# A decoder layer's first stage: eight value blocks copied to places of their own, and five products on zeros ahead of the first data

## The chip, the cores and the metric

The kernel runs on one core of one Trainium2 chip. The metric is the device time of one execution in microseconds, taken as the median of several. A core has five engines that run their own instruction streams and wait for each other by semaphores: TensorE (PE, with its weight loads shown as PEld), VectorE (DVE), ScalarE (ACT), GpSimd (POOL) and SyncE (SP, which here only issues transfers). All arithmetic is float32 in and out.

## What is computed

The reference is one pre-norm decoder layer on 32 sequences of 64 tokens with 512 features: self-attention with 32 heads, cross-attention with 32 query heads and 8 key/value heads of 128 on the context `ctx_4096`, and a linear layer with low-rank additions, each added to `x`. The part that matters here is the beginning of the cross-attention, which does not need `x` and stands first in the program: keys and values of the context, and the keys' rotary embedding.

```python
k = (key @ Wk).reshape(nb, q_len, KVH, D).transpose(0, 2, 1, 3)      # key = value = ctx, Wk, Wv: 512 x 1024
v = (value @ Wv).reshape(nb, q_len, KVH, D).transpose(0, 2, 1, 3)
cos = cos_t[position_ids][:, None]
sin = sin_t[position_ids][:, None]
k = k * cos + _rotate_half(k) * sin
```

## The kernel before

A float32 product is made of three products of "fp32r" parts: each operand is split into a high part (ACT copies with rounding, `*_hi`) and a low part (DVE subtracts, `*_lo`), and PE sums hi*hi, hi*lo and lo*hi over the four chunks of 128 features (`product3`, lines 75 to 77, twelve instructions of 128x512 each). Where a product is made on plain float32 instead, PE runs every written product as two instructions in the trace: lines 1835 and 1836 write 4 x 4 products of 256 columns for `p_ps_qk` and `p_ps_s` (NCH = 4 terms, KC = 4 chunks).

The first stage is class `KeysAndValues`. The 2048 tokens stand in four blocks of 512 (`NB`), the keys in 8 heads of 128 (`KVH`), and the values of a block in eight value blocks: 4 tiles of 128 tokens by 2 halves of 512 features. Every engine has a `first()` for block 0 and a `body(b)` for blocks 1 to 3; the order of the work is written out by hand in them.

For block 0 PE runs, in this order:
- `first_values` (lines 444 to 446): value blocks 0 to 3, chunk by chunk as context and weights come in, 48 instructions into four PSUM banks;
- `values(0, i)` for i = 4 to 7. Blocks 4 and 5 wait for `v_copied` of 1 and 2, blocks 6 and 7 for 5 and 6, since they write banks that blocks 4 and 5 used;
- `keys(0, 0)` and `keys(0, 1)`;
- after `id_in` and `row_in` (line 460: all 16 gathers of rotary rows must have landed) 32 transposes (line 465), four for each of eight halves of a cosine or sine table, in two banks by turns, each after ACT has copied out the one two before;
- `keys(0, i)` for i = 2 to 7.

ACT in block 0 copies value block i out of PSUM (`copy_values`, line 330) and after each splits key weights i (line 320), then copies the eight table parts (line 345), then splits the context of block 1 (line 309). `v_out` has two buffers: copy i waits for `v_stored[i % 2]`, that is, until the store of copy i - 2 into `v_scratch` has landed. SP issues, in order: the first context and value weights, eight key-weight loads (line 239, after `c_ready` of 4), eight stores of values (line 256), the context load of block 1 (line 271, 1 MB), and then stores of keys (line 251) and loads of `x`. POOL gathers the 16 sets of rotary rows (line 298), one behind the other, after the last value weight has landed. DVE makes the low parts, then `rotate(b, i)` (lines 169 to 171), which needs both table parts of its block; between the first rotations stand the four `context_lo(1, c)`.

`cos_t` and `sin_t` are two tables of 128 x 2048 each in SBUF. They are written first by the ACT copies of line 345, and read from `rotate(0, 0)` on.

Of the kernel before, what the change touches and what calls it, by code (L numbers as in the profile page):

```python
# [26 lines left out]
P = 128  # L27
# [146 lines left out]
class KeysAndValues:  # L174

    def __init__(self, nc, m, base, banks, x, norm1, ident, drams, wv1_hi, wv1_lo):
        x_dram, ident_dram, pos_dram, table_dram, ctx_dram, wk_dram, wv_dram, wv1_dram, k_scr, v_scr, cos_scr, sin_scr = drams
        NKV = KVH * D2
        NH = NKV // BLOCK  # L180
        KB = 1024

        def sb(name, at, shape, dt=F32):
            return nc.alloc_sbuf_tensor_at("p1_" + name, shape, dt, offset=base + at)
# [17 lines left out]
        def rows(t):  # L202
            return rows_of[t // (3 * TPB)][:, t % (3 * TPB), :]

        def values_bank(b, i):

            return ps_k[i % 2] if b == 0 and 2 <= i < TPB else ps_v[i % 2]
# [9 lines left out]
        c_part, c_ready = m.sem("p1_c_part"), m.sem("p1_c_ready")  # L217
        k_done, v_done, k_terms, k_added, v_copied = (m.sem("p1_" + n) for n in ("k_done", "v_done", "k_terms", "k_added", "v_copied"))
        k_stored, v_stored = [m.sem(f"p1_k_stored{i}") for i in range(2)], [m.sem(f"p1_v_stored{i}") for i in range(2)]
        wv1_in, wv1_part, wv1_ready = (m.sem("p1_" + n) for n in ("wv1_in", "wv1_part", "wv1_ready"))  # L220
        self.k_stored, self.tables_out, self.v_done, self.c_ready = k_stored, tables_out, v_done, c_ready
        self.row_copied, self.wv1_ready = row_copied, wv1_ready
# [7 lines left out]
        def sync(sp):  # L230
# [22 lines left out]
            def store_values(b, i):  # L253
                need(sp, v_copied, b * KVH + i + 1)
                t, g0 = i % TPB, (i // TPB) * (KVH // NH)
                sp.dma_start(v_scr[g0:g0 + KVH // NH, ds(b, 1), :, t, :].rearrange("g b p d -> p (g b) d"),
                             v_out[i % 2][:, :].rearrange("p (g d) -> p g d", d=D2)).then_inc(v_stored[i % 2], 16)

            def first():
                for i in range(KVH):  # L260
# [46 lines left out]
        def scalar(act, extra):  # L307
            def context_hi(b, c):
                nc.scalar.activation(c_hi[b % 2][:, c, :], c_raw[b][:, c, :], ACT.Copy).then_inc(c_part, 1)

            def value_weights_hi(n):
                h, c = n // KC, n % KC
                act.wait_ge(v_raw_in[n], 16)
                cols = slice(h * BLOCK, (h + 1) * BLOCK)
                nc.scalar.activation(w_hi["v"][:, c, cols], raw["v"][:, c, cols], ACT.Copy).then_inc(part_hi["v"], 1)

            def key_weights_hi(i):
                act.wait_ge(k_raw_in[i // 2], 32)
                cols = slice(i * D2, (i + 1) * D2)
                nc.scalar.activation(w_hi["k"][:, :, cols], raw["k"][:, :, cols], ACT.Copy).then_inc(part_hi["k"], 1)  # L320

            def own_value_weights_hi(c):
                need(act, wv1_in, 16)
                need(act, v_done, (NB - 1) * KVH)
                nc.scalar.activation(wv1_hi[:, c, :], wv1_raw[:, c, :], ACT.Copy).then_inc(wv1_part, 1)

            def copy_values(b, i):
                need(act, v_done, b * KVH + i + 1)
                need(act, v_stored[i % 2], (b * (KVH // 2) + i // 2) * 16)
                nc.scalar.activation(v_out[i % 2][:, :], values_bank(b, i)[:, :], ACT.Copy).then_inc(v_copied, 1)  # L330

            def first():
                for c in range(KC):
                    act.wait_ge(c_in0[c], 16)
                    context_hi(0, c)
                    value_weights_hi(c)
                for c in range(KC):
                    value_weights_hi(KC + c)
                for i in range(KVH):
                    copy_values(0, i)  # L340
                    key_weights_hi(i)
                for n in range(2 * NB):
                    act.wait_ge(row_turned, n + 1)
                    dst = (cos_t, sin_t)[n % 2]
                    nc.scalar.activation(dst[:, (n // 2) * BLOCK:(n // 2 + 1) * BLOCK], ps_r[n % 2][:, :], ACT.Copy).then_inc(row_copied, 1)
                act.wait_ge(c_in, 16)
                for c in range(KC):
                    context_hi(1, c)

            def body(b):  # L350
                for i in range(KVH):
                    if not (b == NB - 1 and i == KVH - 1):
                        copy_values(b, i)
                    if b + 1 < NB and i == 1:
                        need(act, c_in, (b + 1) * 16)
                        need(act, k_done, b * KVH)
                        need(act, v_done, b * KVH)
                    if b + 1 < NB and i % 2 == 1:
                        context_hi(b + 1, i // 2)
                    if b == NB - 1 and 1 <= i <= KC:  # L360
                        own_value_weights_hi(i - 1)
                    extra(b, i)
            blocks(first, body)
            copy_values(NB - 1, KVH - 1)

        def vector(dve, extra):
# [25 lines left out]
                rotate_terms(nc, ps_k[i % 2], cos_t[:, ds(b * BLOCK, BLOCK)], sin_t[:, ds(b * BLOCK, BLOCK)], k_out[i % 2], rb[i % 2]).then_inc(k_terms, 1)  # L392

            def first():
                for c in range(KC):
                    context_lo(0, c)
                    value_weights_lo(c)
# [24 lines left out]
        def tensor(pe, extra):  # L422
# [12 lines left out]

            def first_values():

                for c in range(KC):
                    pe.wait_ge(c_ready, c + 1)
                    pe.wait_ge(ready["v"], c + 1)  # L440
# [1518 lines left out]
```

## Time and profile before

| | us |
|---|---|
| median of three runs | 1444.82 |
| lowest and highest | 1443.29, 1449.35 |
| the profiled execution | 1440.5 |
| its span in the trace | 1438.7 |
| PE busy in the span | 1397.2 |
| first product of PE at | 5.99 |
| first transposed rotary rows at | 39.19 |

All rows below come from the one profiled execution. Times in them are microseconds from the start of its span; the span leaves out 1.8 us of the 1440.5. "PEclk" is the granted clock of TensorE as a share of its full 2.4 GHz, so 0.50 is 1.2 GHz; where no product runs, the column reads 1.00 and tells nothing. A product is shown with its full latency and the next starts before it ends, so the pace of PE is the distance of two starts.

### The profile page before, as it was taken

Reading aid. Unit: us, or ns where it says so; the run is one execution under the profiler, and the core shown is the slowest. Engines: PE = TensorE matmul, PEld = TensorE weight load, DVE = VectorE, ACT = ScalarE, POOL = GpSimd, SP = SyncE. Lnnn points to the kernel's source line nnn. Section 1 sums busy time; section 2 is a strip of 40 time slices with the busy share of each in tenths; the row PEclk is TensorE's granted clock in tenths of the full one; section 3 lists DMA queues with packets and bytes.
Section 4 is the critical chain, followed back from the end, with each engine's and each line's share of the span. In section 5 each row is a group of like instructions: output and inputs, shape, how many; then the busy total and the mean of one; then the engine's idle time right before and its main releaser. Section 6 shows DMA issues by size and latency. Waiting matters only on the chain.

```text
span 1438.7 us, 27956 instructions
## 1 busy us (share of the span) xinstructions
PE 1397.2 (97%) x11616; PEld 1157.2 (80%) x11616; DVE 1023.3 (71%) x1470; ACT 429.9 (30%) x731; POOL 521.1 (36%) x459
## 2 busy tenths in 40 slices
PE   7999999999998889999999999999999999999999
PEld 6788888788886678888888888888888888878787
DVE  3655552789889877777777767768768768778754
ACT  4111233656657422122122112122122122121421
POOL 4322220433444434344344344344344344342231
PEclk9999999999999999999999999999999999999999
DMA  8565330000005101011011011012011011003011
GB/s 262 160 202 183 103 103 1 3 17 25 10 3 154 52 15 45 30 44 48 28 45 51 24 45 58 17 45 59 16 45 60 15 45 59 16 15 115 1 59 59
DMA packets 79116, 84.09 MB, mean 58 GB/s; under 512 B 9824, under 2 KB 50928, under 8 KB 78736
## 3 DMA queue, kind: packets, MB, share of 16 engines
q1 hardware_dynamic: 68976, 63.42, 14.1%
q10 hardware_dynamic: 9216, 16.78, 3.7%
q0 software_dynamic: 800, 2.11, 0.5%
q8 instruction: 94, 1.54, 0.5%
q14 instruction: 30, 0.25, 0.1%
HBM read 59.22 MB, written 23.07 MB: 57 GB/s over the span
## 4 chain that ended last, share of the span: by engine, by line
PE 84%; DVE 8%; issue 3%; ACT 2%; POOL 1%; DMA 1%; ACTq 0%; SPq 0%; DVEq 0%
PE p_ps_qk L75 6%; PE p_ps_qk L77 6%; PE p_ps_qk L76 6%; PE p_ps_y L1233 6%; PE p_ps_y L1234 6%; PE p_ps_y L1235 6%; PE p_ps_s L75 5%; PE p_ps_s L76 5%; PE p_ps_s L77 5%; PE p_ps_s L1194 3%; PE p_ps_o L75 3%; PE p_ps_o L76 3%; PE p_ps_o L77 2%; PE p_ps_s L1205 2%; PE p_ps_s L1220 2%
## 5 line engine op out<-in xcount | busy, mean ns | idle before, releaser
L1583 POOL TENSOR_TENSOR p_q_rot<-p_q_rot,p_rb 128x512 f32<-128x512 f32 x128 | 165.3, 1291 | 341.2 <-DVE p_rb L171 341.2
L1233 PE MATMUL p_ps_y<-p_wo_hi,p_o_hi 128*128 128x512 f32 x384 | 150.2, 391 | 1.3 <-DVE p_o_lo L1464 1.3
L1234 PE MATMUL p_ps_y<-p_wo_lo,p_o_hi 128*128 128x512 f32 x384 | 149.4, 389 | 0.0
L1235 PE MATMUL p_ps_y<-p_wo_hi,p_o_lo 128*128 128x512 f32 x384 | 149.4, 389 | 0.0
L75 PE MATMUL p_ps_qk<-p_xt_hi,p_wq_hi 128*128 128x512 f32 x312 | 131.2, 421 | 1.0 <-DVE p_xt_lo L1488 1.0
L77 PE MATMUL p_ps_qk<-p_xt_hi,p_wq_lo 128*128 128x512 f32 x312 | 123.6, 396 | 0.0
L76 PE MATMUL p_ps_qk<-p_xt_lo,p_wq_hi 128*128 128x512 f32 x312 | 122.6, 393 | 0.0
L1000 POOL TENSOR_TENSOR p_pn<-p_p,p_inv 128x512 f32<-128x512 f32 x64 | 66.1, 1064 | 154.2 <-DVE p_inv L890 151.6
L1473 DVE TENSOR_TENSOR x_sb<-p_ps_y,x_sb 128x512 f32<-128x512 f32 x96 | 66.3, 691 | 70.6 <-PE p_ps_y L1235 69.7
L1332 ACT ACTIVATE p_pt_hi<-p_ps_s 128x512 fp32r<-128x512 f32 x64 | 38.1, 599 | 235.3 <-PE p_ps_s L1205 235.2
L1338 ACT ACTIVATE p_o_hi<-p_ps_s 128x512 fp32r<-128x512 f32 x64 | 34.8, 596 | 242.8 <-PE p_ps_s L1220 242.8
L304 POOL TENSOR_TENSOR p_k_out<-p_k_out,p_rb 128x512 f32<-128x512 f32 x32 | 44.8, 1400 | 116.5 <-DVE p_rb L171 116.5
L1233 PEld LDWEIGHTS p_ps_y<-p_wo_hi,p_o_hi 128*128 128x128 f32 x384 | 72.1, 188 | 16.7 <-DVE p_o_lo L1464 1.5
L1235 PEld LDWEIGHTS p_ps_y<-p_wo_hi,p_o_lo 128*128 128x128 f32 x384 | 72.1, 188 | 15.0
L1234 PEld LDWEIGHTS p_ps_y<-p_wo_lo,p_o_hi 128*128 128x128 f32 x384 | 72.1, 188 | 15.0 <-issue 0.2
L1589 POOL TENSOR_TENSOR p_v_lo<-p_v_in,p_v_hi 128x512 fp32r<-128x512 f32 x32 | 42.6, 1330 | 114.0 <-ACT p_v_hi L1323 114.0
L1576 POOL TENSOR_TENSOR p_s<-p_s,p_inv 128x512 f32<-128x512 f32 x64 | 65.5, 1044 | 34.7 <-DVE p_inv L1440 34.7
L1327 ACT ACTIVATE p_s<-p_s 128x1024 f32<-128x1024 f32 x32 | 34.0, 1062 | 139.1 <-DVE p_s L1432 139.1
L169 DVE TENSOR_TENSOR p_q_rot<-p_ps_qk,p_cos_t 128x512 f32<-128x512 f32 x64 | 43.9, 686 | 41.7 <-PE p_ps_qk L77 41.7
L77 PEld LDWEIGHTS p_ps_qk<-p_xt_hi,p_wq_lo 128*128 128x128 f32 x312 | 59.1, 189 | 13.9
L75 PEld LDWEIGHTS p_ps_qk<-p_xt_hi,p_wq_hi 128*128 128x128 f32 x312 | 59.4, 190 | 13.3 <-DVE p_xt_lo L1488 1.4
L1194 PE MATMUL p_ps_s<-p_k_t,p_q_rot 128*64 128x64 f32 x2048 | 66.8, 224 | 2.2 <-POOL p_q_rot L1583 2.2
(262 smaller groups left out, 3790.6 us busy)
## 6 DMA issues: line engine op xcount, KB each, us to landing
v_scratch<-p_v_out SPq DMA_DIRECT2D x32, 256.0 KB, 2.8
k_scratch<-p_k_out SPq DMA_DIRECT2D x32, 256.0 KB, 2.1
p_raw<-in_wq SPq DMA_DIRECT2D x32, 256.0 KB, 3.1
p_raw<-in_wo SPq DMA_DIRECT2D x32, 256.0 KB, 2.6
p_k_t<-k_scratch ACTq DMA_DIRECT2D x32, 256.0 KB, 2.6
p_v_in<-v_scratch ACTq DMA_DIRECT2D x32, 256.0 KB, 2.8
x_sb<-in_x SPq DMA_DIRECT2D x16, 256.0 KB, 3.0
out<-p_y SPq DMA_DIRECT2D x16, 256.0 KB, 2.0
```

The lines of the kernel that those rows point to most:

```text
L75: nc.tensor.matmul(out, lh, rh, start=(c == 0), stop=False)
L76: nc.tensor.matmul(out, lh, rl, start=False, stop=False)
L77: mm = nc.tensor.matmul(out, ll, rh, start=False, stop=(c == last))
L304: nc.gpsimd.tensor_tensor(k_out[i % 2][:, :], k_out[i % 2][:, :], rb[i % 2][:, :], ALU.add).then_inc(k_added, 1)
L1000: nc.gpsimd.tensor_tensor(pn[:, u * PB:(u + 1) * PB, :, :].rearrange("p b j k -> p j b k"), part, scale.unsqueeze(3).broadcast_to([P, HALF ...
L1194: mm = nc.tensor.matmul(ps_s[half][rows, (h // PAIR * UB + j) * SEQ:(h // PAIR * UB + j + 1) * SEQ], q_rot[:, h, cols], k_t[:, cols], star ...
L1233: nc.tensor.matmul(ps_y[t][:, :], oh, w_hi["o"][h][:, :], start=(h == 0), stop=False)
L1234: nc.tensor.matmul(ps_y[t][:, :], oh, w_lo["o"][h][:, :], start=False, stop=False)
L1235: mm = nc.tensor.matmul(ps_y[t][:, :], ol, w_hi["o"][h][:, :], start=False, stop=(h == H - 1))
L1473: nc.vector.tensor_tensor(x[:, tile, :], ps_y[t][:, :], x[:, tile, :], ALU.add).then_inc(y_added, 1)
L1576: nc.gpsimd.tensor_tensor(part, part, inv[:, half * SETS:(half + 1) * SETS].unsqueeze(2).broadcast_to([P, SETS, SEQ]), ALU.mult).then_inc( ...
L1583: nc.gpsimd.tensor_tensor(q_rot[:, h, :], q_rot[:, h, :], rb[:, :], ALU.add).then_inc(q_added, 1)
```

## The change

Three edits in block 0 of the first stage, and two semaphore lines that go with them:

1. The copies of value blocks 0 to 7 no longer go to the two `v_out` buffers but to eight pieces of 512 columns of the tables `cos_t` (blocks 0 to 3) and `sin_t` (blocks 4 to 7), and don't wait for earlier stores. The stores read from there.
2. Before its first table copy (n = 0) ACT waits until all eight stores have landed (`v_stored` of 64 on both semaphores).
3. DVE's first instruction clears `v_out[0]`, and PE, before anything else, waits for that and runs five products of 128 x 256 columns on it, in plain float32, into the bank `ps_r[0]`, which nobody reads until the transposes overwrite it.

```diff
+        WARM = 5
...
+        def values_out(b, i):
+
+            return (cos_t, sin_t)[i // TPB][:, i % TPB * BLOCK:(i % TPB + 1) * BLOCK] if b == 0 else v_out[i % 2][:, :]
...
+        blank = m.sem("p1_blank")
...
                 sp.dma_start(v_scr[g0:g0 + KVH // NH, ds(b, 1), :, t, :].rearrange("g b p d -> p (g b) d"),
-                             v_out[i % 2][:, :].rearrange("p (g d) -> p g d", d=D2)).then_inc(v_stored[i % 2], 16)
+                             values_out(b, i).rearrange("p (g d) -> p g d", d=D2)).then_inc(v_stored[i % 2], 16)
...
             def copy_values(b, i):
                 need(act, v_done, b * KVH + i + 1)
-                need(act, v_stored[i % 2], (b * (KVH // 2) + i // 2) * 16)
-                nc.scalar.activation(v_out[i % 2][:, :], values_bank(b, i)[:, :], ACT.Copy).then_inc(v_copied, 1)
+                if b > 0:
+                    need(act, v_stored[i % 2], (b * (KVH // 2) + i // 2) * 16)
+                nc.scalar.activation(values_out(b, i), values_bank(b, i)[:, :], ACT.Copy).then_inc(v_copied, 1)
...
                 for n in range(2 * NB):
                     act.wait_ge(row_turned, n + 1)
+                    if n == 0:
+                        for i in range(2):
+                            act.wait_ge(v_stored[i], 16 * KVH // 2)
...
             def first():
+                nc.vector.memset(v_out[0][:, :], 0.0).then_inc(blank, 1)
                 for c in range(KC):
                     context_lo(0, c)
...
             def first_values():
 
+                pe.wait_ge(blank, 1)
+                for _ in range(WARM):
+                    nc.tensor.matmul(ps_r[0][:, 0:BLOCK // 2], v_out[0][:, 0:P], v_out[0][:, 0:BLOCK // 2], start=True, stop=True)
                 for c in range(KC):
```

PE at its start, before: the products of `first_values` are the first thing behind its entry branch (`p_ps_s` are four PSUM banks, `p_c_hi_67` the high part of the context of block 0).

```order
0 L588 UNCONDITIONAL_BRANCH
1 L444 MATMUL p_ps_s<-p_wv_hi,p_c_hi_67 128x512
2 L445 MATMUL p_ps_s<-p_wv_lo,p_c_hi_67 128x512
3 L446 MATMUL p_ps_s<-p_wv_hi,p_c_lo_69 128x512
4 L444 MATMUL p_ps_s<-p_wv_hi,p_c_hi_67 128x512
```

PE at its start, now (`p_ps_y` holds `ps_r`, `p_v_out_71` is `v_out[0]`; lines are those of the changed file).

```order
0 L602 UNCONDITIONAL_BRANCH
1 L451 MATMUL p_ps_y<-p_v_out_71 128x256 x5
2 L458 MATMUL p_ps_s<-p_wv_hi,p_c_hi_67 128x512
3 L459 MATMUL p_ps_s<-p_wv_lo,p_c_hi_67 128x512
4 L460 MATMUL p_ps_s<-p_wv_hi,p_c_lo_69 128x512
```

Five written products stand ahead of the first on data; nothing else moved on PE.

ACT in block 0, from the third copy of values to the first table copy, before, with the semaphores that each waits for.

```order
L330 ACTIVATE p1_v_out0_71<-p3_ps_s 128x512 [waits p3_p1_v_stored0,p3_p1_v_done]
L320 ACTIVATE p1_wk_hi_64<-p1_raw_k_53 128x4x128 [waits p3_p1_k_raw_in1]
L330 ACTIVATE p1_v_out1_72<-p3_ps_s 128x512 [waits p3_p1_v_stored1,p3_p1_v_done]
L320 ACTIVATE p1_wk_hi_64<-p1_raw_k_53 128x4x128 [waits p3_p1_k_raw_in1]
L330 ACTIVATE p1_v_out0_71<-p3_ps_s 128x512 [waits p3_p1_v_stored0,p3_p1_v_done]
...
L330 ACTIVATE p1_v_out1_72<-p3_ps_s 128x512 [waits p3_p1_v_stored1,p3_p1_v_done]
L320 ACTIVATE p1_wk_hi_64<-p1_raw_k_53 128x4x128 [waits p3_p1_k_raw_in3]
L345 ACTIVATE p1_cos_t_55<-p3_ps_y 128x512 [waits p3_p1_row_turned]
L345 ACTIVATE p1_sin_t_56<-p3_ps_y 128x512 [waits p3_p1_row_turned]
```

The same stretch of ACT now.

```order
L337 ACTIVATE p1_cos_t_55<-p3_ps_s 128x512 [waits p3_p1_v_done]
L326 ACTIVATE p1_wk_hi_64<-p1_raw_k_53 128x4x128 [waits p3_p1_k_raw_in1]
L337 ACTIVATE p1_cos_t_55<-p3_ps_s 128x512 [waits p3_p1_v_done]
L326 ACTIVATE p1_wk_hi_64<-p1_raw_k_53 128x4x128 [waits p3_p1_k_raw_in1]
L337 ACTIVATE p1_sin_t_56<-p3_ps_s 128x512 [waits p3_p1_v_done]
...
L337 ACTIVATE p1_sin_t_56<-p3_ps_s 128x512 [waits p3_p1_v_done]
L326 ACTIVATE p1_wk_hi_64<-p1_raw_k_53 128x4x128 [waits p3_p1_k_raw_in3]
L355 ACTIVATE p1_cos_t_55<-p3_ps_y 128x512 [waits p3_p1_v_stored1,p3_p1_v_stored0,p3_p1_row_turned]
L355 ACTIVATE p1_sin_t_56<-p3_ps_y 128x512 [waits p3_p1_row_turned]
```

The order is the same; the waits on stores moved from the copies to the first table copy.

## Rows read from the trace of the kernel before

**Rows 1.** The page, part 1: busy us (share of the span), instructions.

```profile
PE 1397.2 (97%) x11616; PEld 1157.2 (80%) x11616; DVE 1023.3 (71%) x1470; ACT 429.9 (30%) x731; POOL 521.1 (36%) x459
```

**Rows 2.** Stretches: start:end, length, busy of PE, PEld, DVE, ACT, POOL, PEclk, DMA, GB/s.

```profile
27.00:28.00 1.00, 1.00 (x5) 0.81 (x4) 0.69 (x1) 0.63 (x3) 0.73 (x1) 0.76 0.55 156
39.00:44.00 5.00, 4.36 (x33) 3.33 (x32) 2.07 (x3) 3.42 (x7) 0.80 (x1) 1.00 0.16 64
47.00:61.00 14.00, 11.97 (x51) 9.15 (x51) 11.80 (x18) 0.03 (x1) 7.18 (x5) 1.00 0.46 149
61.00:200.00 139.00, 139.00 (x620) 114.67 (x619) 79.23 (x132) 24.31 (x42) 38.55 (x29) 1.00 0.48 156
```

**Rows 3.** The chain that ended last, 17 to 27 us: start, us, what.

```profile
17.85 4.57 DMA v_scratch<-p_v_out
...
23.13 2.71 DMA v_scratch<-p_v_out
...
26.58 0.50 PE p_ps_s L75
```

**Rows 4.** Timeline, first products and last low part: start, us, engine, line [idle, releaser].

```profile
5.99 0.76 PE L444 MATMUL p_ps_s<-p_wv_hi,p_c_hi 128*128 128x512 f32 x1 [5.99 <-DVE p_wv_lo L375]
...
6.98 0.63 PE L446 MATMUL p_ps_s<-p_wv_hi,p_c_lo 128*128 128x512 f32 x1
7.41 0.63 PE L444 MATMUL p_ps_s<-p_wv_hi,p_c_hi 128*128 128x512 f32 x1
...
10.66 0.40 PE L446 MATMUL p_ps_s<-p_wv_hi,p_c_lo 128*128 128x512 f32 x1
10.85 0.69 DVE L375 TENSOR_TENSOR p_wv_lo<-p_raw_v,p_wv_hi 128x512 fp32r<-128x512 f32 x1
```

**Rows 5.** Timeline of PE, from the first stall to the transposes.

```profile
24.28 0.39 PE L77 MATMUL p_ps_s<-p_wv_hi,p_c_lo 128*128 128x512 f32 x1
26.58 0.50 PE L75 MATMUL p_ps_s<-p_wv_hi,p_c_hi 128*128 128x512 f32 x1 [1.91 <-ACT p_v_out L330]
...
31.02 0.39 PE L75 MATMUL p_ps_s<-p_wv_hi,p_c_hi 128*128 128x512 f32 x1
...
39.19 1.03 PE L465 MATMUL p_ps_y<-ident,p_rows 128*128 128x128 f32 x8
40.48 1.15 PE L465 MATMUL p_ps_y<-ident,p_rows 128*128 128x128 f32 x8 [0.25 <-ACT p_cos_t L345]
```

**Rows 6.** The last gather of rotary rows: its issue, its landing, the landings of all 16.

```profile
33.04 0.95 POOL L298 DMA_INDIRECT p_rows<-in_table_c,p_pos  x1 [0.30 <-issue]
...
p_rows<-in_table_c,p_pos POOLq DMA_INDIRECT x1, 2.7
...
DMA to landing us min/median/max: 2.7/3.8/4.8
```

**Rows 7.** SP's first issue; a DVE memset; plain float32 products of 256 columns, PE.

```profile
0.75 0.38 SPq L232 DMA_DIRECT2D p_raw_k<-in_ctx  x1
...
L1772 DVE MEMSET p_a_hi<- 128x512 f32 x1 | 0.5, 485 | 0.1
...
1327.76 1.99 PE L1835 MATMUL p_ps_qk<-p_pick,p_la 128*128 128x256 f32 x8
```

**Rows 8.** Other idle times of PE, and the granted clock after the first of them.

```profile
448.00 0.77 PE L75 MATMUL p_ps_y<-p_wo_hi,p_o_hi 128*128 128x512 f32 x1 [2.81 <-DVE x_sb L901]
...
507.31 0.63 PE L163 MATMUL p_ps_y<-ident,p_xn 128*128 128x128 f32 x4 [2.09 <-DVE p_xt_lo L1488]
...
448.00:454.00 6.00, 6.00 (x76) 4.79 (x77) 5.89 (x9) 3.49 (x7) 5.04 (x5) 0.50 1.23 258
```

**Rows 9.** Timeline: eight transposes at half clock; two rows on keys(0, 2).

```profile
266.72 1.94 PE L628 MATMUL p_ps_s<-ident,p_pn 128*128 128x128 f32 x8 [0.95 <-DVE p_s L881]
...
46.70 0.39 PE L77 MATMUL p_ps_s<-p_c_hi,p_wk_lo 128*128 128x512 f32 x1
48.84 0.69 DVE L169 TENSOR_TENSOR p_k_out<-p_ps_s,p_cos_t 128x512 f32<-128x512 f32 x1
```

## The prediction

> **What bounds the kernel now.** I read the page first: PE is busy for 97% of the span [rows 1], so only what keeps PE waiting, or slows it, can be won. Then the stretches [rows 2]: from 61 to 200 us PE is busy for 139.0 of 139 us, so whatever the first stage gains or loses by then is handed on as it is. In the first 61 us PE loses time at four places. It starts at 5.99, when DVE has made the first low part [rows 4]. Its first ten or so products stand 0.43 apart (6.98 to 7.41), which is 1.2 GHz, and only from about 10.5 do they come closer, down to 0.227, as the 36 steps from 31.02 to 39.19 show, which is 2.4 GHz [rows 4, 5]. At 24.51 the next value block should start, and starts at 26.58, behind ACT's copy [rows 5]. The chain says what that copy waited for: two stores into v_scratch, of 4.57 and 2.71 us, with one copy between them [rows 3]. After this stall the clock falls: 0.76 on average in the 28th microsecond [rows 2], and the twelve products from 26.58 to 31.02 take 4.44 us [rows 5]. The transposes then start at 39.19 [rows 5]. Behind them the path is the table copies on ACT, the split of the next context and the rotations on DVE, POOL and the key stores, with PE waiting 2.03 us in all from 47 to 61 [rows 2]: that part starts when the transposes start, not when PE is ready.
>
> **What each edit gives PE.** The edits on the copies: without the wait for stores the gap from 24.51 to 26.58 goes, 2.07 us. Block 6 then needs copies 0 to 4, and the key-weight splits between them work on loads issued before any store; I cost that at nothing, and at up to the 2.07 if those loads were late. With the gap goes the fall of the clock: 4.44 less 12 x 0.227 = 1.72 us.
>
> The products on zeros: the nearest row for one of them is the plain float32 product of 256 columns at line 1835. There 16 written products show as 32 records, and the seven steps in the group of eight are (1.99 - 0.38) / 7 = 0.23 each at full clock [rows 7]. So one written product is two of these, 0.46, and at half clock, where PE stands at its start, about 2 x 0.43 = 0.86; five are 4.3 us. DVE's memset of 128x512 takes 0.485, and the engines are let go by 0.75, when SP issues its first load [rows 7]. So PE can start at about 1.4 and is through at 5.7, before the 5.99 at which data comes: nothing is added. If the memset came 0.7 later it would add 0.4. The clock rose 4.5 us after PE's first product at 5.99, and 4.4 us after its restart at 26.58 [rows 4, 5]; after the restart at 448.00 it was still at 0.50 six microseconds later [rows 8]. From 1.4 that gives 5.9 to 7.9 or so. The 71 steps from 5.99 to the product at 24.28 took 18.29 us against 71 x 0.227 = 16.12 [rows 4, 5], so the zeros win up to 2.2 us, and 1.2 with the late rise. DVE's low parts come fast enough for full speed: the last of the first four chunks is made by 10.85 + 0.69 = 11.5 [rows 4], and PE would want it at 5.99 + 36 x 0.227 = 14.2. I take 1.7.
>
> Sum for PE: 2.07 + 1.72 + 1.7 = 5.5 (5.0 to 6.0), so PE would be ready for the transposes at 33.7 in place of 39.19.
>
> **What comes late next.** The transposes also wait for all 16 gathers of rotary rows (line 460), and the change leaves these where they are: POOL issues the last one at 33.04, one each 1.25 us, from the landing of the last value weight on. It landed 2.7 us after its issue, at 35.7; the 16 took 2.7 to 4.8, with a median of 3.8 [rows 6]. Before, PE came 3.4 us after the last of them, so this wait did not show. Now it ends last, and it caps the whole change: at 35.7 to 37.8, plus 0.2 to wake PE. The last gather was the fastest because little else ran; now the 1 MB context load, which SP issues behind the eighth store, moves some five microseconds ahead with that store, to about 29, and runs beside it. So I take a landing between the best and the median, 3.25, or 36.3, and the transposes at 36.5: 2.7 us earlier than 39.19. By the Trainium skill, "DMA: Bandwidth & Descriptors", section "Issuing engines are not separate DMA queues", transfers share the same 16 engines and interleave whoever issues them; that speaks for such a delay, and no row of before shows this pair of transfers together.
>
> ACT's new wait for all eight stores lies behind this. Block 7 is done 24 products before the transposes, at 33.7 - 5.4 = 28.3, its copy (0.6) at 28.9, and a store takes 2.71 to 4.57 us [rows 3], so 31.6 to 33.5: some three microseconds before the first table part can be copied. Queued behind that wait are only the table copies, whose data isn't there. SP's context load moves earlier with the stores; its reader stands behind the table copies.
>
> **The price of the new wait.** PE now stands idle from 33.7 to 36.5, 2.8 us. In the trace the clock fell after idle times of 1.91 and 2.81 us and did not after one of 2.09 [rows 5, 8]; 2.8 is at the upper of these, so I take a fall. At half clock eight transposes take 1.94 us against 1.15 [rows 5, 9]. The tables are turned in pairs of banks with a period of 40.48 - 39.19 = 1.29 us, and four of the eight transposes stand on the path of a period, so a pair costs 0.4 more. A fall over two to four pairs is 0.7 to 1.6 us; I take 1.0. Key product 2 behind them has slack: it ended at 47.1 and DVE took it up at 48.84 [rows 9].
>
> So the forecast is -2.7 + 1.0 = -1.7 us: the span goes from 1438.7 to 1437.0, the profiled execution from 1440.5 to 1438.8. The median of the runs stands 4.3 above the profiled execution, so 1443.1.
>
> **The rivals.**
> - The gathers hold PE, but the clock stays up, as after the 2.09 us. For it: the idle time is in two minds of the rows. Time: -2.7, 1442.1. A zero-product part that does nothing for the clock ends here too: PE is then ready at 35.4, waits 1.1 us for the same gathers, less than any idle time after which a row shows a fall, and the time is again -2.7. The five products would then be worth nothing.
> - The gathers come early enough, since less stands in their way from 18 to 28 us, and PE goes on at 33.7. Time: -5.5, 1439.3. Against it: the issue at 33.04 alone forbids it, unless POOL issues faster.
> - Half clock through all transposes and into the keys. The rows before speak against: with only transposes from 39 to 44 PEclk stayed 1.00 [rows 2]. But there the clock was up already. If it stays down the transposes cost 1.6, and keys(0, 2) takes 12 x 0.43 = 5.1 instead of 2.7; 1.7 of the extra 2.4 fits in the slack, so 0.7 more. Time: -2.7 + 1.6 + 0.7 = -0.4, 1444.4. By the Trainium skill, "TensorE: Matmul & The Clock Gate", section "Part 4: PE-mode transpose", transposes don't count as activity of PE, so that the full clock doesn't engage on them; the trace does not agree for a clock that is up, and no row shows it for one that is down at this place.
> - Slower: the last gather is held up by the context load and the stores that now run together. Its place is the row wait of line 460; with the 1.6 for a long fall, the change loses from a landing of 4.4 us on (33.04 + 4.4 + 0.2 + 1.6 = 39.2), which is below the longest of the 16, 4.8. With 5.5 us it is +1.1, or 1446.0.
>
> **How the numbers follow.** Forecast 0.45; clock stays up or zeros idle 0.24; all arrives 0.06; half clock long 0.13; late gather 0.12. The predicted time is the forecast's, 1443.1. The cases span 1439.3 to 1446.0. The three runs before lie 1.5 below to 4.5 above their median, so a median of as few can be off by some 1.5 either way: 1438.5 to 1447.5 leaves out less than 2 in 10. About 0.5%, 7.2 us, is what a measurement of this kernel can tell from no change. No case reaches it by itself; only the spread of the medians could add to the fastest or the slowest. So faster 0.04, same 0.93, slower 0.03.
>
> **What would show it.** Right: one group of products from about 1.4 to 5.7 ahead of the first on data; 0.227 steps from 6 to 8 us on and no gap at 24.5; the eighth value copy at about 28.4; PE idle from 33.7 until the last gather lands near 36, the first transposes at 36.5; PEclk 0.5 in some microseconds from 36 to 42; and beyond 61 the same picture, 1.7 earlier. The steps on the products are wrong if PE's first data product starts later than 6.1 or the steps are 0.43 beyond 8. The cap is wrong if the transposes start before 35.7. The whole is wrong if the gap at 24.5 stays, because ACT waits for key weights instead of stores, or if a wait beyond 61 takes the gain back.

## The result and the profile after

The changed kernel takes 1447.08 us in the median of 22 runs, the kernel before 1444.03 in as many on the same chips: a ratio of 1.0020, interval 1.0012 to 1.0028. One of the 22 runs took 3872 us, for no reason that is known; it does not move the median. The forecast was 1443.1, 1.7 us below the median of the first three runs of before, 1444.82. It is 3 us slower instead: within the 0.5% and inside the range, but on the other side. The profiled spans are 1444.5 and 1438.7.

First the stretches of the changed kernel, in the columns of [rows 2]; with them the six microseconds from 20 on:

```profile
20.00:26.00 6.00, 6.00 (x28) 4.98 (x27) 2.28 (x4) 2.72 (x5) 4.78 (x5) 1.00 1.12 355
27.00:28.00 1.00, 1.00 (x6) 0.81 (x5) 0.00 (x0) 0.48 (x1) 0.75 (x1) 1.00 0.67 236
39.00:44.00 5.00, 4.49 (x21) 3.78 (x22) 1.78 (x3) 2.39 (x4) 0.00 (x0) 0.50 0.43 166
44.00:46.00 2.00, 1.88 (x14) 1.50 (x14) 0.28 (x1) 1.58 (x3) 1.27 (x1) 0.92 0.00 0
61.00:200.00 139.00, 138.63 (x616) 114.07 (x615) 80.15 (x132) 23.20 (x41) 39.09 (x29) 1.00 0.49 159
```

The gap at 24.5 us and the low clock behind it are gone (PE busy 6.00 of 6, PEclk 1.00 in the 28th microsecond, 0.76 in [rows 2]). But from 39 to 44, where the transposes stand, PEclk is 0.50 in place of 1.00. And from 20 to 26 the transfers move 355 GB/s; in the kernel before it was 271:

```profile
20.00:26.00 6.00, 4.67 (x21) 3.54 (x19) 1.46 (x3) 2.31 (x5) 4.48 (x6) 1.00 0.93 271
```

The start of PE in the changed kernel (timeline), which answers to [rows 4]:

```profile
1.47 4.63 PE L451 MATMUL p_ps_y<-p_v_out 128*128 128x256 f32 x10 [1.47 <-DVE p_v_out L405]
7.22 0.47 PE L458 MATMUL p_ps_s<-p_wv_hi,p_c_hi 128*128 128x512 f32 x1 [1.12 <-DVE p_wv_lo L385]
7.53 0.40 PE L459 MATMUL p_ps_s<-p_wv_lo,p_c_hi 128*128 128x512 f32 x1
7.76 0.39 PE L460 MATMUL p_ps_s<-p_wv_hi,p_c_lo 128*128 128x512 f32 x1
7.99 0.39 PE L458 MATMUL p_ps_s<-p_wv_hi,p_c_hi 128*128 128x512 f32 x1
```

The zero products run from 1.47 to 6.10, and the first products on data stand 0.23 apart, not 0.43. The first of them comes at 7.22 instead of 5.99, because its value weight landed later. I don't take this for work of the change, which leaves these loads alone: the kernel before, run again, had it at 6.46, and kernels with zero products below at 6.42, 6.20 and 6.62. Of all the kernels below only e7, with 5.93, starts earlier than the trace that I forecast from.

The chain that ended last (start, us, what), and the transposes with the idle time ahead of them, which answer to [rows 5] and [rows 6]:

```profile
33.07 0.95 POOL p_rows L304
34.32 5.05 DMA p_rows<-in_table_c,p_pos
39.51 4.71 PE p_ps_y L479 x20
```

```profile
39.51 6.60 PE L479 MATMUL p_ps_y<-ident,p_rows 128*128 128x128 f32 x32 [4.83 <-DMA p_rows<-in_table_c,p_pos]
```

PE was ready at 34.7 and waited 4.83 us for the last gather, which was issued 1.3 us later than before and landed 5.05 us after its issue, not 2.7. Then come 32 transposes in 6.60 us. From the DVE instructions of both traces, matched one by one, I take the **offset** of a kernel, its start less that of the kernel before: +1.8 us at 47 us, and the same +1.8 until 271. By 300 it is +3.95, and at 400 +4.2. In between, this stands in PE's timeline. The kernel before has from 262 to 345 us no idle time of PE put down to "issue", which is time in which the engine waited for nothing that the profile shows:

```profile
274.51 1.57 PE L627 MATMUL p_ps_s<-p_k_x,p_q_x 32*64 32x64 f32 x127 [0.33 <-ACT p_q_x L751]
277.60 0.27 PE L627 MATMUL p_ps_s<-p_k_x,p_q_x 32*64 32x64 f32 x1 [1.51 <-issue]
...
292.17 0.39 PE L77 MATMUL p_ps_qk<-p_xt_hi,p_wk_lo 128*128 128x512 f32 x1 [0.95 <-issue]
```

This is the self-attention, whose code the change does not touch. So there are two questions: what the first stage lost, and what stands behind 271 us. The offsets of before run again say how far they can be trusted: -0.3 between 271 and 400 us, but +2.1 between 400 and 515, and most of the other kernels show that too. There the first trace of before was lucky, and I don't read that stretch.

### The profile page after: what moved, and what is told of

Its sections match the earlier page's. It is cut to its first block, busy times and chain, and to the rows that moved or that the text cites. A ratio compares the mean times of both kernels' runs of the same rounds, so it can differ in the third digit from the quotient of the medians.

```text
span 1444.5 us, 27972 instructions
## 1 busy us (share of the span) xinstructions
PE 1398.2 (97%) x11626; PEld 1157.6 (80%) x11626; DVE 1024.3 (71%) x1471; ACT 430.3 (30%) x731; POOL 521.5 (36%) x459
## 4 chain that ended last, share of the span: by engine, by line
PE 82%; DVE 8%; issue 3%; POOL 2%; ACT 2%; DMA 1%; SPq 0%; ACTq 0%; DVEq 0%; POOLq 0%
PE p_ps_qk L75 6%; PE p_ps_qk L77 6%; PE p_ps_qk L76 6%; PE p_ps_y L1247 6%; PE p_ps_y L1248 6%; PE p_ps_y L1249 6%; PE p_ps_s L75 5%; PE p_ps_s L76 5%; PE p_ps_s L77 5%; PE p_ps_s L1208 3%; PE p_ps_o L75 3%; PE p_ps_o L76 3%; PE p_ps_o L77 3%; PE p_ps_s L1219 2%; PE p_ps_s L1234 2%
```

## The experiments

Each run was compared with the kernel before on the same chip (1442.3 us for the first four, 1442.4 for the next four, 1442.9 and 1441.9 for the last two groups). The table sums up what the sections show one by one. "Entries" counts the MATMUL and LDWEIGHTS records that a kernel adds to PE's stream ahead of 271 us. A written plain float32 product is four of them, two and two. "Stalls" is the idle time of PE put down to "issue" between 271 and 400 us, with the number of times (those of 0.2 us or more). The ratio is the recorded one of the paired runs, not the quotient of the medians.

| kernel | entries | median us | ratio (interval) | offset at 271 | growth 271 to 400 | stalls |
|---|---|---|---|---|---|---|
| after | 20 | 1447.1 | 1.0020 (1.0012 to 1.0028) | +1.9 | +2.4 | 2.5 (2) |
| e5 before again | 0 | 1443.4 | 1.0013 (1.0003 to 1.0022) | +0.4 | -0.3 | 0 |
| e1 copies only | 0 | 1443.8 | 1.0006 (0.9997 to 1.0015) | +3.6 | -0.8 | 0 |
| e2 zeros only | 20 | 1447.8 | 1.0033 (1.0020 to 1.0046) | +0.7 | +3.0 | 2.3 (2) |
| e3 five tiny | 20 | 1446.9 | 1.0036 (1.0023 to 1.0050) | +1.2 | +4.8 | 2.9 (3) |
| e4 two wide | 8 | 1443.4 | 1.0003 (0.9994 to 1.0012) | +0.5 | +0.9 | 0 |
| e6 context behind | 20 | 1445.1 | 1.0018 (1.0005 to 1.0030) | -0.1 | +1.9 | 2.3 (2) |
| e7 gathers early | 20 | 1445.2 | 1.0027 (1.0015 to 1.0039) | +1.3 | +1.6 | 1.7 (2) |
| e8 early, two wide | 8 | 1441.9 | 1.0000 (0.9991 to 1.0009) | -1.4 | +0.9 | 0.7 (1) |
| e9 copies, early | 0 | 1443.5 | 0.9999 (0.9989 to 1.0009) | +1.6 | +0.1 | 0.3 (1) |
| e10 before, early | 0 | 1444.6 | 1.0008 (0.9997 to 1.0018) | +0.7 | +0.4 | 0 |
| e11 ten tiny | 40 | 1454.8 | 1.0073 (1.0058 to 1.0088) | +2.1 | +11.3 | 6.5 (5) |
| e12 five tiny late | 0 | 1443.7 | 1.0008 (0.9996 to 1.0020) | +0.4 | +1.7 | 0 |
| e13 twenty tiny | 80 | 1468.4 | 1.0172 (1.0151 to 1.0192) | +7.2 | +19.6 | 12.3 (8) |
| e14 sixty-four tiny | 256 | 1462.2 | 1.0136 (1.0119 to 1.0153) | +18.9 | +1.7 | 0 |

The e5 row is the yardstick: an unchanged kernel reads 1.0013. So the ratios of e1, e4 and e8 to e12, but for e11, are no difference that these runs can tell, and e6 is barely one.

The growth alone is a weak sign. Kernels without a stall have -0.8 to +1.7, as much as e6 and e7 have with two stalls. One thing that differs between such traces is how long PE stands at half clock between 262 and 400 us: not at all in the changed kernel, e1, e6, e7 and e9; 3.4 us in before, e2, e4, e5, e8 and e10; 6.8 us in e3, e12 and e14; 10.2 us in e11 and e13. The last column is the surer sign.

### One part alone

e1 is the changed kernel without the memset and the zero products:

```diff
-                nc.vector.memset(v_out[0][:, :], 0.0).then_inc(blank, 1)
-                pe.wait_ge(blank, 1)
-                for _ in range(WARM):
-                    nc.tensor.matmul(ps_r[0][:, 0:BLOCK // 2], v_out[0][:, 0:P], v_out[0][:, 0:BLOCK // 2], start=True, stop=True)
```

> The change without its five products on zeros and without the memset: only the eight value copies to places of their own, with the wait for all stores at the first table copy. PE has the same instructions as before. Theory A (two causes: gathers of rotary rows land late because four value stores and the context load now run beside them, and PE's instruction stream got 20 entries longer, which moves stalls of its own into the loops behind 260 us): the transposes start at 38.5 to 40 instead of 39.19, after an idle PE of 2 to 3 us; no PE wait put down to issue at the products of line 613 or 77 behind 260 us; ratio to the kernel before 0.999 to 1.001. Theory B (copies are harmless or a gain, the zeros' half second of activity is the whole loss): transposes at 36.5 or earlier, ratio 0.998. Theory C (the moved stores alone cost everything, also behind 260 us): ratio 1.002, spans 3 us longer.

Its transposes start later than before and later than expected, at 40.91, at half clock (0.24 us each), after a wait for the gathers; keys(0, 2) comes 3.5 us late. The copies alone win nothing in the first stage; yet behind 271 us nothing is lost, and the medians don't tell its end from that of before (1.0006).

```profile
40.91 4.48 PE L475 MATMUL p_ps_y<-ident,p_rows 128*128 128x128 f32 x19 [4.26 <-DMA p_rows<-in_table_c,p_pos]
```

e2 is the kernel before with those four lines, and nothing of the copies.

> The kernel before with only the memset of v_out[0] and the five products on zeros ahead of the first data. Theory A: the products of the first two chunks run at full clock from 6 to 7 us on, PE waits longer for the third value copy (about 3 us in place of 1.9), transposes at about 38.5 (0.7 earlier), but with 20 more entries in PE's instruction stream the same waits put down to issue as in the changed kernel appear behind 260 us, 3 to 4 us in all; ratio 1.0015 to 1.003. Theory B: same as the kernel before or slower by at most 1 us through the late first data; nothing behind 100 us. Theory C (stores alone): ratio 0.9995.

It has full clock from the first product on data on, but the 1.7 us so won are waited away at the third value copy, 3.72 us in place of 1.91 [rows 5], and behind 271 us both stalls are there, and the growth. The wait in question:

```profile
26.74 0.50 PE L75 MATMUL p_ps_s<-p_wv_hi,p_c_hi 128*128 128x512 f32 x1 [3.72 <-ACT p_v_out L331]
```

e3 is e2 with products of four columns:

```diff
-                    nc.tensor.matmul(ps_r[0][:, 0:BLOCK // 2], v_out[0][:, 0:P], v_out[0][:, 0:BLOCK // 2], start=True, stop=True)
+                    nc.tensor.matmul(ps_r[0][:, 0:4], v_out[0][:, 0:P], v_out[0][:, 0:4], start=True, stop=True)
```

> The kernel before with the memset and five products on zeros of only 4 columns each: the same 20 additional entries in PE's instruction stream as in the changed kernel, but no PE time to speak of (under 0.5 us, long before the first data) and no effect on the clock. Theory A (length of the stream decides): PE waits put down to issue behind 260 us as in the changed kernel, ratio 1.002 to 1.003. Any theory that lays the loss behind 260 us on the clock, the copies or the transfers: the same as the kernel before, ratio 1.000 (0.9995 to 1.0005), no such waits.

These take 2.30 us, not the 0.5 expected, end at 3.76 and do nothing for the clock: the products on data start at 6.30, at half clock, as before. Still the kernel is slower by as much as e2, with its stalls. So neither the zeros' work nor the early clock is what costs, but that the instructions are there. Of its growth of 4.8 us the stalls are 2.9; 3.4 us more at half clock than in before come with it. e4 is the changed kernel with two zero products of 512 columns, 8 entries in place of 20:

```diff
-        WARM = 5
+        WARM = 2
-                    nc.tensor.matmul(ps_r[0][:, 0:BLOCK // 2], v_out[0][:, 0:P], v_out[0][:, 0:BLOCK // 2], start=True, stop=True)
+                    nc.tensor.matmul(ps_r[0][:, :], v_out[0][:, 0:P], v_out[0][:, :], start=True, stop=True)
```

> The changed kernel with two products on zeros of 512 columns in place of five of 256: 8 additional entries in PE's instruction stream instead of 20, about 3.4 us of PE at half clock instead of 4.3. Theory A: the first stage as in the changed kernel (transposes at 38.5 to 40), while the waits put down to issue behind 260 us lie elsewhere or are gone: the sum of them differs from the changed kernel's 3.3 us by at least 1 us; ratio 0.999 to 1.002. Theories without the stream's length: the same as the changed kernel, ratio 1.002.

The first products on data run at full clock as with five, no stall stands in the loops behind 271 us, and the loss is gone. A gain is not there either: its last gather, issued at 34.96, lets the transposes start at 38.49.

### The first stage

e5 is the kernel before, unchanged.

> The kernel before once more, unchanged, for a second profile. If the waits put down to issue behind 260 us hang on PE's instruction stream (theory A), they lie where they lay in the first profile (none at the products of lines 613 and 77). The first data product may start anywhere from 6.0 to 6.5 us; transposes between 39 and 40.5; ratio 1.000.

Its trace gives the spread used above. e6 holds the 1 MB context load back until the gathers have landed, in the changed kernel:

```diff
+                sp.wait_ge(row_in, 16 * TILES)
                 load_context(1)
```

> The changed kernel with one more wait: SP holds the 1 MB load of the next context until all 16 gathers of rotary rows have landed. Theory A1 (the last gather lands late because it runs beside that load): it lands 2.7 to 3.5 us after its issue instead of 5.05, the transposes start at 37.5 to 38.5 instead of 39.5, the context is in at 43 to 44, before ACT wants it at 45; the ratio to the kernel before falls from 1.002 by about 0.001. Theory A2 (the stores alone hold the gathers up): landing still about 5, transposes at 39.5, ratio 1.002.

```profile
38.15 4.68 PE L480 MATMUL p_ps_y<-ident,p_rows 128*128 128x128 f32 x24 [4.16 <-DMA p_rows<-in_table_c,p_pos]
```

The last gather was issued at 35.3, a microsecond later than in the changed kernel (34.3), and yet the transposes start 1.4 us earlier: it landed 2.7 us after that issue, as in [rows 6]. So it was the context load, issued at 35.05 in the changed kernel, that made 5.05 of 2.7. The other traces agree. Where the load was issued between 1.9 us before the last gather and 0.8 us after it, the gather took 4.3 to 6.9 us to land (e12 4.27, the changed kernel 5.05, e1 6.56, e9 6.89). Where it came 3.1 us before or earlier, or 1.5 us after or later, it took at most 3.8 (before 2.70, e3 2.80, e2 3.22, e4 3.39, e10 3.54, e8 3.75).

And why was the load issued at 35.05 and not near 29, as forecast? SP issues it behind the eighth store, and the eighth value copy came late. ACT and SP of the changed kernel, and SP of e4, where the copy came at 28.24:

```profile
33.95 0.60 ACT L337 ACTIVATE p_sin_t<-p_ps_s 128x512 f32<-128x512 f32 x1 [5.32 <-remote]
35.05 0.43 SPq L277 DMA_DIRECT2D p_raw_v<-in_ctx  x1
...
29.34 0.43 SPq L277 DMA_DIRECT2D p_raw_v<-in_ctx  x1
```

"remote" says only that the profile names nobody who ended the wait. It need not be the work of the change, for the unchanged kernel e5 has such a copy as well:

```profile
37.55 0.60 ACT L330 ACTIVATE p_v_out<-p_ps_s 128x512 f32<-128x512 f32 x1 [4.66 <-remote]
```

What held these copies stays open. e7 lets POOL begin its gathers after four raw value blocks instead of sixteen, e8 does the same in e4:

```diff
-            for n in range(NH * KC):
+            for n in range(KC):
                 pool.wait_ge(v_raw_in[n], 16)
```

> The changed kernel with POOL's gathers let go after the first four value-weight loads instead of all eight. Theory A (the gathers cap the gain of the first stage): the last gather is issued at about 30 and lands by 35, PE goes on to the transposes at 34.5 to 35.5 without an idle time that matters and without half clock, 4 to 5 us earlier than in the changed kernel; behind 260 us the waits put down to issue stay (3 us); ratio 0.9985 to 1.000. If something else held the transposes (ACT's wait for the stores, the table copies), they stay at 38 or later and the ratio at 1.002.

> The kernel of the run with two products of 512 columns on zeros, with the gathers let go early as well. Theory A with both of its causes taken away: transposes at 34 to 35, waits put down to issue behind 260 us of about 1 us as in that run; ratio to the kernel before 0.996 to 0.998, so 3 to 5 us faster. If only one cause was real the ratio stays at 0.9985 to 1.000.

```profile
39.86 4.97 PE L479 MATMUL p_ps_y<-ident,p_rows 128*128 128x128 f32 x24 [2.61 <-ACT p_cos_t L355]
```

```profile
36.80 3.42 PE L479 MATMUL p_ps_y<-ident,p_rows 128*128 128x128 f32 x16 [2.69 <-DMA p_rows<-in_table_c,p_pos]
40.37 1.18 PE L479 MATMUL p_ps_y<-ident,p_rows 128*128 128x128 f32 x8 [0.16 <-ACT p_cos_t L355]
```

In e7 the first eight transposes start at 36.22, but then another wait took the place of the gathers: the first table copy waits for the last of the eight stores, because the seventh value copy came at 34.54, after 8.09 us of idle time put down to "remote", and the eighth at 35.56 instead of 28 to 29. In e1, e4, e6 and e8 no copy was held like this. In e8 the eighth copy was in time, and the transposes start at 36.80, the only case in which the first stage gains: -1.4 us at 271, near the -1.7 of the forecast. It is not the 34 to 35 of my expectation, and of the 3 to 5 us that I expected at the end nothing shows for sure: 1441.9 against 1442.4, 1.0000. This kernel has one stall, 0.68 us at 275.39.

The same edit without zero products, on e1 and on the kernel before:

> The eight value copies without the zero products, and the gathers of the rotary rows wait for the first four raw value blocks only, instead of all sixteen: the two edits that each did no harm or gained in the first stage, without the added entries in PE's instruction stream. Theory A (the copies lose because their stores, the context load and the gathers share the DMA engines, and the gathers end last; 1.0006 for the copies alone): begun near 11.5 us instead of 13.9, the last gather is issued near 31 to 32 us and lands by 36 to 37, transposes start at 37 to 38 instead of 40.9, keys(0,2) 3 us earlier than with the copies alone; no issue stall above the common one in the loops behind 260 us except the one of about 0.9; ratio 0.998 to 0.9995, 1440 to 1441.5 us. Theory B (only the length of PE's stream moves the end, what the first stage gains is waited away later): ratio 1.000 to 1.001, as for the copies alone.

> The kernel before with one edit: the gathers of the rotary rows wait for the first four raw value blocks only. Theory A (gathers cap the first stage only where copies have made PE ready early): PE is held by the third and fourth value copy (26.7 us) and reaches its transposes at about 36.5 us as before; the gathers are done by 34 to 35, so transposes start at 36.5 to 37.5 instead of 39.2, but the stores of v_scratch lie now beside the gathers, so the copy that waits for them may come up to 1 us later: gain 0.5 to 2.5 us at 46 us, ratio 0.9985 to 1.0. Rival: the gathers, begun at 11.5 us, take DMA time from the raw value blocks and from the stores on which the third copy waits, and PE's gap at 26 us grows by as much as is gained behind: ratio 1.000 to 1.001.

e9 has its transposes at 38.95 against 40.91 in e1, with keys(0, 2) 2 us earlier, but nearly all at half clock; less than the 3 us expected, and no gain in time. In e10 the transposes stay about where they were, at 39.84. My expectation of 36.5 was a slip: in the kernel before, PE reaches them at 39.19 without a wait for gathers, so earlier gathers can't help. Its idle time at the third copy is as before, 1.90 us.

### Behind 271 us

Three runs ask what the 20 entries do. e11 has ten of e3's tiny products instead of five. e12 puts five of them behind the loops, on operands that are there:

```diff
                 need(pe, pt_ready, 2 * it)
+                if it == 0:
+                    for _ in range(5):
+                        nc.tensor.matmul(ps_s[0][0:SEQ, 0:4], q_rot[:, 0, 0:SEQ], k_t[:, 0:4], start=True, stop=True)
```

> The kernel before with the memset and ten plain products of four columns ahead of the first value product, where the earlier run had five: 40 more entries in PE's stream instead of 20, with next to no work of their own. Theory B1 (each entry ahead of the loops brings PE's stream closer to running dry: the stall grows with their number): issue stalls behind 260 us sum to 5 us or more beside the common one, ratio 1.005 to 1.008, about 1449 to 1453 us. Theory B2 (the place where a block of the stream begins against a loop decides, so that any shift can be good or bad): stalls of 0 to 4 us without order in the number, ratio 0.9995 to 1.004, and what five entries more brought need not grow. Idle time of the first stage should be as with five: first products at half clock, transposes from about 40 us.

> The kernel before with five plain products of four columns, on operands that are there, at the head of the score products of the third stage (486 us), behind the loops at 275 to 302 us where the stalls stood. The same 20 entries, on the same engine, later. Theory B (entries ahead of a loop move where the stream is fetched against it): nothing changes ahead of 486 us, no issue stall at 275 to 302 us, ratio 0.9995 to 1.001; what may come is one or two stalls of about 1 us in loops behind 486 us. Rival (the stream's length as a whole, or the number of products, is the cost, wherever they stand): stalls as with the five tiny products in front, ratio 1.003 to 1.004.

e12 has no stall from 262 to 400 us and no loss (1.0008). e11 loses 11.9 us, which is what theory B1 (each entry costs) foretold and more than I had allowed theory B2. Its first stalls stand here:

```profile
275.61 1.49 PE L618 MATMUL p_ps_s<-p_k_x,p_q_x 32*64 32x64 f32 x117 [0.33 <-ACT p_q_x L742]
278.21 0.36 PE L618 MATMUL p_ps_s<-p_k_x,p_q_x 32*64 32x64 f32 x11 [1.10 <-issue]
...
292.91 0.49 PE L618 MATMUL p_ps_s<-p_k_x,p_q_x 32*64 32x64 f32 x7 [1.71 <-issue]
...
309.22 0.32 PE L618 MATMUL p_ps_s<-p_k_x,p_q_x 32*64 32x64 f32 x2 [1.76 <-issue]
```

The score products come in runs of 128, and the stall cuts one: 127 and 1 in the changed kernel, 117 and 11 here. Twenty entries more, which are ten products (one MATMUL and one LDWEIGHTS each), moved it forward by ten products. So it stands at a fixed place of the stream. From pass to pass it moves back by some four and a half products, 11, 7, 2, and then leaves the run. Counted over all of PE's own records in the trace (products, weight loads, and what its sequencer does), the first stall of every kernel that has one stands ahead of record 3266, and the next ones at 3777, 4290, 4801 and so on, 511 to 513 apart. The page tells what such a place can be. Of the changed kernel, part 1 and part 3 (queue, kind: packets, MB, share):

```profile
PE 1398.2 (97%) x11626; PEld 1157.6 (80%) x11626; DVE 1024.3 (71%) x1471; ACT 430.3 (30%) x731; POOL 521.5 (36%) x459
...
q8 instruction: 94, 1.54, 0.4%
```

> The kernel before with the memset and twenty plain products of four columns ahead of the first value product: 80 entries more in PE's stream. They last near 9 us from 1.5 us on, at 0.44 us each, so the first data product comes 4 to 5 us later and this is taken off by the offset at 200 us. What counts is the growth of the offset to the kernel before between 271 and 400 us: 11.3 us with 40 entries, 1.6 to 4.7 with 20. Theory B1 (each entry costs): 22 us or more. Theory B2 (the place of a block's beginning decides): the stall in the run of 128 small products at 278 us stands about 31 products before the run's end instead of 11, there is again about one a run or less, each 1 to 2 us, and the growth is 5 to 15 us.

> The kernel before with the memset and sixty-four plain products of four columns ahead of the first value product: 256 entries more, one block of 16 KB if an entry is 64 bytes. They last near 28 us at 0.44 us each, so everything behind comes some 22 to 24 us later, less what the first stage waits for anyway; that is taken off by the offset at 200 us. Theory B1 (each entry costs): the offset grows by far more than the 11.3 us of 40 entries between 271 and 400 us, 70 us by the line through 40. Theory B2 (the place of a block's beginning decides, and a whole block more puts each back where it was): no stall in the runs of small products at 278 to 340 us, growth of -1 to +2 us, as in the kernel before and the others with no entry ahead.

```profile
279.87 1.25 PE L618 MATMUL p_ps_s<-p_k_x,p_q_x 32*64 32x64 f32 x97 [0.33 <-ACT p_q_x L742]
282.35 0.49 PE L618 MATMUL p_ps_s<-p_k_x,p_q_x 32*64 32x64 f32 x31 [1.23 <-issue]
...
296.61 0.47 PE L618 MATMUL p_ps_s<-p_k_x,p_q_x 32*64 32x64 f32 x27 [1.37 <-issue]
...
311.08 0.45 PE L618 MATMUL p_ps_s<-p_k_x,p_q_x 32*64 32x64 f32 x22 [1.48 <-issue]
```

With 80 entries the run is cut into 97 and 31, as foretold, and then at 27, 22, 18, 13, 9 and 4: seven passes meet a stall in their run where e11 had three (e11 has two more and e13 one more by 400 us, among the wide products). I had not thought of the number of passes when I wrote 5 to 15 us; 19.6 is more, and by itself near the other theory's 22. The stalls are not the whole growth: they are 6.5 of 11.3 us in e11 and 12.3 of 19.6 in e13. Behind some of the longer ones the clock fell to 0.50 for 3.4 us (at 292.8 and 309.9 in e11, behind 1.71 and 1.76 us idle). The rest I did not break down. The run with 256 entries decides: its waits of PE show only these for "issue" (in total, times, longest us), the first of them in every kernel,

```profile
PE p_ps_s L1225 <- issue: 2.1, 1, 2.1
PE p_ps_qk L75 <- issue: 0.3, 1, 0.3
```

and its growth is +1.7 us against 19.6 with fewer entries. The 18.9 us that it loses come from the products themselves, which last until 28.9. More entries are not what costs; where a block of the stream begins is, and the distance after which the pattern returns, 256 entries in 16 KB, makes an entry 64 bytes.

The traces have the start of each of the 94 packets, and they tie the stalls to them. From 271 to 430 us nine kernels have 27 such stalls. Every one of them ends 2.25 to 2.87 us after the start of a 16 KB fetch, 1.24 to 1.56 us after that packet was through. In the changed kernel the fetches start at 274.94 and 289.91 us, and the stalls end at 277.60 and 292.17. At 274.94 PE had 175 records to go to record 3266, and the run of small products passes them in 1.1 us. In the kernel before the fetch starts at 274.33, with 98 to go, most of them slower; PE is at record 3266 at 276.70, 2.4 us after the fetch began, just in time; e9, which has the same stream on PE, was caught there by 0.34 us. So a stall is PE waiting for a block whose fetch began less than 2.3 to 2.9 us before it was wanted. What decides when a fetch begins these runs don't show. And not all "issue" time is this: the changed kernel has 0.94 us of it at 468.72, 12 us behind the last fetch.

## Why the prediction was wrong

**The products on zeros: right in size, blind for what they are.** 4.63 us against 4.3 forecast, over before data came, full clock at once. That "nothing is added" was wrong: the sum held their time and not their place in PE's stream. This term was missing altogether, and no rival held it. Its two stalls measured 2.5 us in the changed kernel, where the offset grew by 2.4 between 271 and 400 us; in e3, whose products do no work worth the name, the stalls are 2.9 us. e4 does the same warming with 8 entries, has no stall there, and ends level with before.

**The gap and its clock: right.** Both went, and PE was ready at 34.7: the forecast's 33.7, and most of the 1.2 by which the data came late.

**The cap by the gathers: right in kind, mis-sized.** I took a landing of 3.25 us after an issue at 33.04. It was 5.05 after 34.32, and the transposes started at 39.51 instead of 36.5: +1.3 for the issue and +1.8 for the landing. The issue came later because POOL began at 14.30 instead of 13.84 and three of its issues took 1.16 to 1.27 us instead of 0.95, while the transfers moved 355 GB/s. How much of that the change did is not shown: the kernels with the old copies issued the last gather anywhere from 33.0 to 34.6 (e5 at 33.79, e12 at 34.58), those with the new ones and no early gathers at 34.2 to 35.3, and the trace that I forecast from is the earliest of all these. The landing came later because the context load ran beside it, which e6 shows. In the kernel before SP issued that load at 35.05 too, but there the last gather, 2.0 us older, had nearly landed; now it was 0.7 us old. I had expected the load at 29, from an eighth value copy at 28.4 to 28.9. That copy came at 33.95, for a reason that stays open, and this is what set the load beside the gather. Where it was in time, in e4, the load was issued at 29.34 and the gather landed after 3.39 us, close to my 3.25. The rival "slower" named this place and decided at 4.4 us; it had 0.12 and is what happened.

**The price of the wait: a little low.** The clock fell, after 4.8 us idle and not 2.8, and about twenty of the 32 transposes ran at half clock (4.71 us in the chain): together they took 1.5 us more than before, where I had 1.0 out of 0.7 to 1.6.

Put together: -1.7 forecast, +3.1 for the gathers, +0.5 for the clock, gives +1.9 at 271 us, measured +1.8 to 1.9. Then +2.4 for the stream. That is 4.3 in one profiled execution, of which the medians show 3.1. That the measured time lies inside my range is no merit of the working: the range was wide enough for both signs.

**The ACT wait for eight stores** had three microseconds to spare in my working. It had them in e4, e6 and e8; in e7 the late seventh and eighth copies used them up.

## What to carry to other kernels

An edit that adds a few instructions ahead of a tight loop is not free because the engine was idle there: look in the profile for idle time put down to "issue" in loops far behind the edit, and, if it is there, change the number of entries (fewer, wider instructions) before giving up the edit. A stretch of stores, gathers and loads that the old kernel kept apart by its waits will meet when the waits go; take the landing times for the sum from the slow end of what the trace shows, and the issue times from more than one trace.

## What the runs showed of the hardware

- PE's stream can stall where a 16 KB block of it (256 entries) begins, if PE comes there less than 2.3 to 2.9 us after the fetch of the block began. In these loops that happened at every second block, in or just behind a run of 128 small products. A stall inside a run is 0.8 to 2.0 us, and its place in the run moves by one product for every two entries put ahead of it. A change of 20 entries at 1.5 us made the first one at 277.6 us.
- A gather of rotary rows landed at most 3.8 us after its issue, and 4.3 to 6.9 us when a 1 MB load was issued within two microseconds before it or 0.8 behind it.
- The start of the first product on data differed from kernel to kernel by 1.3 us (5.93 to 7.22, without e13 and e14, whose zero products stood in its way), with the same loads in the same order: too much to forecast a microsecond from one trace.
- Only transposes ran in e8 from 36.80 to 40.22, after 2.69 us idle, and during them the granted clock rose:

```profile
37.00:40.00 3.00, 3.00 (x16) 2.60 (x15) 0.53 (x1) 1.48 (x3) 0.00 (x0) 0.54 0.00 0
41.00:44.00 3.00, 2.84 (x19) 2.28 (x19) 0.57 (x1) 2.72 (x6) 1.26 (x1) 1.00 0.06 23
```

  The columns are those of [rows 2]; eight transposes took 1.18 us from 40.37 on, which is 2.4 GHz. In the changed kernel too the clock was 0.50 until 44 and 0.92 from 44 to 46, while nothing but transposes ran on PE. So the rule of the Trainium skill that I weighed in the prediction ("TensorE: Matmul & The Clock Gate", section "Part 4: PE-mode transpose"), that transposes don't bring the full clock, does not hold for these rows.
